# Row addresses on SyncE and ScalarE: 16 and 8 registers per load, used without a copy

## What is computed

```python
h = jnp.maximum(_layernorm(x, axis=-1), 0.0)
agg = jax.ops.segment_sum(h[src], dst, num_segments=N)   # 200000 edges
z = (1.0 + eps_gin) * h + agg
t = jax.nn.relu(_batchnorm(jnp.dot(z, W1) + b1, g1, bt1))
conv_out = jnp.dot(t, W2) + b2
out = x + jax.nn.relu(_batchnorm(conv_out + h, g2, bt2))
```

## Time and profile before

| | us |
|---|---|
| median of 3 runs | 2220.93 |
| lowest and highest | 2217.61, 2221.61 |
| profiled execution, its own time | 2220.37 |
| its span, first to last instruction | 2218.5 |
| mean granted TensorE clock, share of full speed | 0.816 |
| busy in the span: PE, PEld | 1443.6, 921.4 |
| busy in the span: DVE, ACT, POOL | 1183.5, 1136.8, 1462.8 |

### The profile page before, as it was taken

How to read it: one execution, slowest core, us unless ns; L and a number is a source line. 1 busy time by engine, 2 the same in 40 slices (tenths; PEclk the granted TensorE clock), 3 DMA queues, 4 the chain that set the end, 5 groups by cost and what they waited for, 6 DMA issues and landing times. The chain is left out here.

```text
span 2218.5 us, 37477 instructions
## 1 busy us (share of the span) xinstructions
PE 1443.6 (65%) x4841; PEld 921.4 (42%) x4841; DVE 1183.5 (53%) x4692; ACT 1136.8 (51%) x2511; POOL 1462.8 (66%) x1559
## 2 busy tenths in 40 slices
PE   2556655666655665765766565665656566579997
PEld 2334433444433443433444344443434344354446
DVE  7455554555554555554555545555544555553346
ACT  5455554555544555554555445555445455464446
POOL 7777776777776777776777776777776777730002
PEclk7778777778887888777778887888777887799999
DMA  5334443344343344343344433434434434438447
GB/s 146 115 116 120 129 133 120 114 135 135 115 127 121 116 134 132 114 130 120 115 133 135 134 112 119 135 116 132 126 113 123 133 116 133 129 120 314 170 141 297
DMA packets 118939, 300.49 MB, mean 135 GB/s; under 512 B 33158, under 2 KB 57176, under 8 KB 112546
## 3 DMA queue, kind: packets, MB, share of 16 engines
q0 software_dynamic: 76656, 212.52, 32.0%
q1 hardware_dynamic: 39196, 84.16, 10.9%
q10 hardware_dynamic: 2838, 1.45, 0.2%
HBM read 258.75 MB, written 39.25 MB: 134 GB/s over the span
## 5 line engine op out<-in xcount | busy, mean ns | idle before, releaser
L513 POOL DMA_INDIRECT arena<-in_x,arena x1507 | 1430.7, 949 | 513.6 <-issue 441.4
L1132 PE MATMUL ps<-arena 128*96 128x256 f32 x3126 | 1002.1, 492 | 729.9 <-ACT arena L939 729.9
L939 ACT ACTIVATE arena<-arena,nb,mv 128x256 f32<-128x256 f32 x1523 | 770.6, 587 | 900.1 <-DVE nb L617 867.9
L1132 PEld LDWEIGHTS ps<-arena 128*96 128x96 f32 x3126 | 661.7, 218 | 1054.6 <-issue 790.3
L549 DVE BATCH_NORM_STATS2 st<-arena 128x6 f32<-128x256 f32 x1523 | 517.5, 412 | 728.5 <-DMA arena<-in_x,arena 590.4
L629 DVE TENSOR_TENSOR arena<-arena,ps 128x768 f32<-128x768 f32 x196 | 185.6, 947 | 4.9 <-PE ps L1132 4.8
L1161 PE MATMUL ps<-arena 128*128 128x512 f32 (+3 forms) x412 | 186.2, 577 | 2.6 <-DVE arena L737 2.6
L1241 PE MATMUL ps<-arena,W2s 128*128 128x512 f32 (+1 forms) x400 | 167.9, 582 | 0.5 <-ACT arena L1085 0.5
L535 POOL DMA_DIRECT2D out<-arena x25 | 13.5, 539 | 226.5 <-DVE arena L895 226.5
L706 DVE TENSOR_TENSOR aggT<-aggT,ps 128x192 f32 x196 | 68.5, 350 | 140.4 <-PE ps L1142 121.6
L556 DVE BATCH_NORM_AGGREGATE mv<-st 128x2 f32<-128x6 f32 x1563 | 121.4, 150 | 1.4 <-issue 0.3
(11 more groups left out here) (86 smaller groups left out, 602.0 us busy)
## 6 DMA issues: line engine op xcount, KB each, us to landing
rl_odd<-in_x SPq DMA_DIRECT2D x3712, 1.0 KB
t_T<-arena SPq DMA_DIRECT2D x24, 1024.0 KB, 13.7
arena<-t_T SPq DMA_DIRECT2D x24, 1024.0 KB, 4.9
arena<-in_x,arena POOLq DMA_INDIRECT x1507
W2s<-in_x ACTq DMA_DIRECT2D x1408, 1.0 KB
arena<-in_x SPq DMA_DIRECT2D x97, 128.0 KB
arena<-in_x SPq DMA_DIRECT2D x23, 512.0 KB, 5.8
out<-arena POOLq DMA_DIRECT2D x23, 512.0 KB, 3.8
```

Source lines behind the costliest of these rows:

```text
L513: nc.gpsimd.indirect_dma_start(out=rows[g % RG][:, k, :], out_offset=None, in_=x[:, :], in_offset=bass.IndirectOffsetOnAxis(ap=at, axis=0) ...
L939: last = S.activation(hrow[g % 2][:, k, :], rows_of(g, k), ACT.Relu, bias=nb[:, g % 2, k:k + 1], scale=mv[:, g % 2, k, 1:2])
L1132: last = T.matmul(win_ps[g % 2], sel[:, g % 2, k, :], hrow[g % 2][:, k, :], start=k == 0, stop=k == n - 1)
```

## The change

SyncE now loads the addresses in pieces of 16 that start at a multiple of 16 of the tile, and a tile has exactly 8 pieces. A pass does two pieces where c is even and three where it is odd (`row_pieces(5c // 2, 5(c+1) // 2)`), that is 32 or 48 rows instead of 40. There are 29 x 8 = 232 pieces. The list of groups comes out the same. ScalarE's pieces stay 8 rows in each step. On both engines `snap` gets `donate=True`: the register that was loaded is used in the address itself, with no copy into another. Registers are allocated for each piece and freed behind it. Besides, the bases are first written to PSUM (`base_ps`, in bank 1) and read from there by L641 and L645. The number of rows and of DMAs on each engine is unchanged.

```diff
--- before.py
+++ after.py
@@ -37,10 +37,10 @@
 XW = Q * D
 X_FIRST = 4
 X_EARLY = 16
-SP_PASS = 40
+SP_HALVES = 5
 ACT_STEP = 8
 ROW_BUFS = 3
-SP_REGS = 20
+PIECE = 16
 ROW_BYTES = 4 * D
 
 
@@ -86,7 +86,7 @@
 
         sp_groups = []
         while True:
-            g = 2 * (ceil(P * (len(sp_groups) + 1), SP_PASS) - 1) + 4
+            g = 2 * (ceil(2 * (len(sp_groups) + 1) * P // PIECE, SP_HALVES) - 1) + 4
             if g >= NG - 4:
                 break
             sp_groups.append(g)
@@ -205,6 +205,7 @@
         t_ps = [ps[:, 4 + b, :] for b in range(TB)]
         tr_ps = [[ps[:, 2 + b, :] for b in (0, 1)], [ps[:, 4 + b, :] for b in (0, 1)]]
         misc_ps = ps[:, 6, :]
+        base_ps = ps[:, 1, 0:NG]
         zero_ps = ps[:, 0, :].rearrange("p (f n) -> p f n", f=DB)
         prm_ps = ps[:, 5, P:P + 18]
         iota_ps = ps[:, 7, 0:W]
@@ -280,6 +281,10 @@
             if act_tile(g, k):
                 return act_rows[act_groups.index(g) % ROW_BUFS]
             return rows[g % RG][:, k, :]
+
+        def row_pieces(first, end, tiles):
+
+            return [divmod(n, P // PIECE) for n in range(first, min(end, tiles * P // PIECE))]
 
         def wait_rows(eng, g):
 
@@ -394,33 +399,27 @@
                                  x[q * QN + 4 * a:q * QN + 4 * b, :].rearrange("(p b k) d -> p b (k d)", b=2, k=2)
                                  ).then_inc(s_x[k], 16)
 
-            regs = [sp.alloc_register(f"row{k}") for k in range(SP_REGS)]
-
             def load_at(j):
                 b, p = divmod(sp_groups[j] * GT + GT - 1, P)
                 sp.dma_start(sp_at[j % 2], at_dram[b, p:p + 1, :]).then_inc(s_spat[j % 2], 16)
 
-            def load_rows(j, e, n):
-                if e == 0:
+            def load_rows(j, m):
+                if m == 0:
                     if j + 1 < len(sp_groups):
                         load_at(j + 1)
                     if j >= ROW_BUFS:
                         sp.wait_ge(s_h, sp_groups[j - ROW_BUFS] + 1)
                     sp.wait_ge(s_spat[j % 2], 16 * (j // 2 + 1))
-                sp.reg_load(regs[0:n], sp_at[j % 2][0:1, e:e + n])
-                for k in range(n):
-                    at = sp.snap(regs[k], min_val=0, max_val=(N - 1) * ROW_BYTES)
-                    sp.dma_start(sp_rows[j % ROW_BUFS][e + k:e + k + 1, :].bitcast(mybir.dt.uint8),
+                regs = [sp.alloc_register(f"row{j}_{m}_{k}") for k in range(PIECE)]
+                sp.reg_load(regs, sp_at[j % 2][0:1, m * PIECE:(m + 1) * PIECE])
+                for k in range(PIECE):
+                    e = m * PIECE + k
+                    at = sp.snap(regs[k], donate=True, min_val=0, max_val=(N - 1) * ROW_BYTES)
+                    sp.dma_start(sp_rows[j % ROW_BUFS][e:e + 1, :].bitcast(mybir.dt.uint8),
                                  x_bytes[bass.ds(at, ROW_BYTES)].rearrange("(p e) -> p e", p=1)
                                  ).then_inc(s_sprows[j % ROW_BUFS], 16)
-
-            def row_pieces(c):
-
-                a, end = c * SP_PASS, min((c + 1) * SP_PASS, P * len(sp_groups))
-                while a < end:
-                    n = min(SP_REGS, end - a, P - a % P)
-                    yield a // P, a % P, n
-                    a += n
+                for reg in regs:
+                    sp.free_register(reg)
 
             sp.wait_ge(s_at, 1)
             sp.dma_start(at_dram.rearrange("b p e -> p b e"), tab_i[0]).then_inc(s_atd, 16)
@@ -431,8 +430,8 @@
                 if c == 0:
                     sp.wait_ge(s_atd, 16)
                     load_at(0)
-                for j, e, n in row_pieces(c):
-                    load_rows(j, e, n)
+                for j, m in row_pieces(SP_HALVES * c // 2, SP_HALVES * (c + 1) // 2, len(sp_groups)):
+                    load_rows(j, m)
 
             def load_t(q, k, r, n=QN):
                 if at_least(q, 2):
@@ -636,13 +635,13 @@
             mean_and_var(0)
 
             dve.wait_ge(s_base, 1)
-            own(V.tensor_scalar(base_f, misc_ps[:, 0:NG], HALF, None, ALU.add))
+            own(V.tensor_scalar(base_ps, misc_ps[:, 0:NG], HALF, None, ALU.add))
             dve.wait_ge(s_iota, 2)
             own(V.tensor_tensor(rel_g, dst_f[:, 0:NE].rearrange("p (g k) -> p g k", k=GT),
-                                base_f.unsqueeze(2).to_broadcast([P, NG, GT]), ALU.subtract))
+                                base_ps.unsqueeze(2).to_broadcast([P, NG, GT]), ALU.subtract))
             own(V.tensor_scalar(iota_ps, iota_w[:, :], -HALF, None, ALU.add))
             selection(0)
-            own(V.tensor_tensor(base_f, base_f, sched, ALU.subtract))
+            own(V.tensor_tensor(base_f, base_ps, sched, ALU.subtract))
 
             own(V.tensor_reduce(chk[:, 0:1], rel, X, ALU.max, apply_absolute_value=True))
             own(V.tensor_reduce(chk[:, 1:2], base_f, X, ALU.min))
@@ -984,27 +983,24 @@
                     S.activation(g_h, g_row, ACT.Relu, bias=g_nb, scale=g_mv[:, 1:2]).then_inc(s_gh, 1)
                 act.wait_ge(s_gend, 1)
 
-            regs = [act.alloc_register(f"act_row{k}") for k in range(ACT_STEP)]
-
             def load_at(j):
                 b, p = divmod(act_groups[j] * GT + GT - 2, P)
                 act.dma_start(act_at[j % 2], at_dram[b, p:p + 1, :]).then_inc(s_actat[j % 2], 16)
 
-            def load_rows(g):
-
-                j, e = divmod((g - 1) * ACT_STEP, P)
-                if j >= len(act_groups):
-                    return
+            def load_rows(j, e):
                 if e == 0:
                     if j + 1 < len(act_groups):
                         load_at(j + 1)
                     act.wait_ge(s_actat[j % 2], 16 * (j // 2 + 1))
+                regs = [act.alloc_register(f"act_row{j}_{e}_{k}") for k in range(ACT_STEP)]
                 act.reg_load(regs, act_at[j % 2][0:1, e:e + ACT_STEP])
                 for k in range(ACT_STEP):
-                    at = act.snap(regs[k], min_val=0, max_val=(N - 1) * ROW_BYTES)
+                    at = act.snap(regs[k], donate=True, min_val=0, max_val=(N - 1) * ROW_BYTES)
                     act.dma_start(act_rows[j % ROW_BUFS][e + k:e + k + 1, :].bitcast(mybir.dt.uint8),
                                   x_bytes[bass.ds(at, ROW_BYTES)].rearrange("(p e) -> p e", p=1)
                                   ).then_inc(s_actrows[j % ROW_BUFS], 16)
+                for reg in regs:
+                    act.free_register(reg)
             act.wait_ge(s_atd, 16)
             load_at(0)
 
@@ -1012,7 +1008,9 @@
                 normalise(g - 1)
                 if g < NG:
                     root(g)
-                load_rows(g)
+                j, e = divmod((g - 1) * ACT_STEP, P)
+                if j < len(act_groups):
+                    load_rows(j, e)
                 if g % 2 == 0 and g >= 4:
                     root_node_tile((g - 4) // 2)
                     if g >= 8:
```

## The result

The changed kernel takes **2165.78 us** (median of 4 runs, 2164.77 to 2167.17) against 2221.27 of the kernel before (2217.61 to 2223.43): ratio 0.9752, 95% interval 0.9735 to 0.9769, so 55.5 us less. The forecast was 2169.0 with 2163 to 2182. The profiled execution took 2164.91 us with a span of 2163.0 us; before it was 2220.37 and 2218.5.

The account below looks back on a forecast made before the run. The prediction took SP as pacemaker, with POOL stalled 52.1 us behind it, and POOL as the next. From the profiled 2220.37 us, minus 52.1, plus 0.7 for late groups, it got 2169.0 us, range 2163 to 2182.

Parts of the forecast that it names:

- What bounds the kernel: Gather: SP's queue never rests and sets the pace; POOL, which waits for it, loses 52.1 us in stalls.
- the 23 us a cycle of the sum: SP's predicted rest per cycle of 32 groups after the change: 289 us of work against POOL's 312.
- The copy: SP's register copy for each fetched row: removal saves 57 ns (34 to 71), 212 us over 3712 rows.
- the third rival: SP's row fetches: the DMA, not the instructions, sets the row period, issue grows to 285 ns; 2228 us, chance 0.04.
- the fourth: SP's row fetches: the change doesn't remove the copy, which appears as another move before the DMA; 2228 us, chance 0.02.
- The pieces: SP's address loads: 232 in place of 209, 7.4 us more work; nothing given to starting at multiples of 16.
- The thin margin: Groups 34, 66, 98, 130, 162 after 48-row passes: 1.5 us late, buffers absorb 2.0; 0.7 us put for all five.
- 1.25: Microseconds from the end of SP's last row issue to DVE's start, read at group 34; used for the lateness.
- First rival: 48-row passes: five groups come 3 to 5 us late, POOL stalls 5 to 15 us; 2173 to 2184, chance 0.17.
- Second rival: POOL's gathers: SP's denser rows on the same DMA engines slow POOL's pace 1%, 19 us; 2188 us, chance 0.06.

## Why the prediction was right

- *What bounds the kernel*: right. SP was the pacemaker, and 52.1 us of POOL's time were stalls that it caused; all of them went. With the copies back they are there again, and taking out the copies alone brings the whole gain. SP rests more than the 23 us a cycle of the sum, 177 us in 5.7 cycles or 31, and in 48 passes, about half of them, not in most.
- *The copy*: 57 ns were taken between 34 and 71; 63 to 65 were measured. The issue kept its 228 ns, so the third rival, that the DMA sets the period, is out, and so is the fourth.
- *The pieces*: nothing was given to them beyond 7.4 us of SP's work. The load of 16 took 1.23 us in the median and not 1.16, and the loads of before, of all sizes, 1.39; all 232 together take 320.0 us against 316.1 for the 209, less than the 7.4 more. Where SP is the pacemaker the new shape costs 13 us, and more from its waits, the one behind the short first pass above all, than from loads. The third and fourth rival put this case at 7.4 us, from loads alone. In the changed kernel all of it was hidden, as foretold.
- *The thin margin*: the outcome is right, with luck, since two errors partly cancel. The pass of 48 rows took 20.2 us (20.6 foretold). The last row counted 353.76 - 351.66 = 2.1 us behind its issue and not 1.25. Together 1.9 us late instead of 1.5, just inside the 2.0 that the sum let the buffers absorb: 0.2 us of stalls instead of 0.7. The 1.25 was one row and a low one: where DVE waits for SyncE's row in the kernel before, it starts 1.1 to 1.8 us behind the issue, in the changed kernel 1.7 to 2.1. From the begin of the issue these are 1.95 to 2.33 us. So here the Trainium skill's roughly fixed 2 us for a DMA (SBUF — State Buffer, The DMA setup-cost knee) was nearer than my row; in the kernel before the same time was 1.35 to 2.0 us, so there the 2 us were its upper end. By that rule I had the lateness at 2.0, near the 1.9 that came, but with a pass that was taken 0.4 too long.
- *The other 4 us*: the profiled execution is 4.1 us under the sum. 0.5 of it is the margin. Most is POOL's pace: its gathers took 1425.0 us in all instead of 1430.7, 5.7 less, and the other profiles show that this does not go with the copies. The sum took POOL's pace to stay the same, so that the time came out below it and not at it is chance: with 5.7 us more it would have been near 2170.6. The start took back 1.3 us (its wait is 2.7 us above a pause and not 1.4), and the chain after the last gather took back 1.6, since its second product starts at 1946.09, 34.2 us behind POOL's last tile instead of 32.6; the rest is tenths:

```profile
1946.09 167.91 PE ps L1239 x400
```

- *First rival, the margin lost*: not here, but half of the copies bring it about, at the predicted groups and in sum of the expected size, 7.4 us. *Second rival, contention*: the pauses stayed at 0.305 us and the gathers at 946.

## What to carry to other kernels

Of two engines that feed the same consumer, look for the one whose queue never waits; that one sets the pace, even if it has no busy time in the profile. What it saves counts only down to the pace of the next one: of the 68 us that the copies cost, 59 were gone with one half of SyncE's copies and ScalarE's, the last 9 with the other half. The sum of the rests doesn't tell that nothing will be missed: with 56 us of rests left the kernel with half of the copies still missed five deadlines, so the longest pass in front of a deadline has to be looked at too.

## What had not been expected of the hardware

On two chips the three kernels that also ran in the ordinary case took 1.45 to 1.56 times as long (the kernel before 3466 and 3441 us against 2221). DMA gathers and DVE's arithmetic were no slower (948 ns, and 517.2 us for all of DVE's statistics against 517.5), but a queue of straight code such as SyncE's had instructions of up to 1.49 us among ones of 29 and 228 ns. Taking out the copies was worth more there: 3480.68 - 3147.00 = 334 us between the changed kernel with and without them (the latter with its bases in SBUF), where the ordinary case has 68. What makes instructions slow there was not found.
